# Late tiles of x loaded again in 32x32 blocks and turned by VectorE inside the scan, with their routing done pair by pair

## What is computed

```python
# layer 0, for each token (xf: x by token, tf: cond of its sequence)
shared = silu(xf @ w1) * (xf @ w3) @ w2
s = sigmoid(concat([xf, tf]) @ router_W)
_, topk_idx = top_k(s + router_bias, 2)
gates = s_sel / (s_sel.sum() + 1e-9)            # 1/2 each where the sum is not over 1e-9
y_e = gelu(xf @ W1e[e]) @ W2e[e]
x = x + (shared + sum of gates * y_e) / 3
# layer 1, for each step t of 512
Z = sigmoid(x_t @ Wxz.T + bxz + H @ Whz.T + bhz)
R = sigmoid(x_t @ Wxr.T + bxr + H @ Whr.T + bhr)
Ht = tanh(x_t @ Wxh.T + bxh + R * H @ Whh.T + bhh)
H = Z * H + (1 - Z) * Ht
x_t = x_t + H @ Whq.T + bhq
```

## Time and profile before

| | us |
|---|---|
| median of 3 runs | 1349.34 (1348.22 to 1351.28) |
| the profiled execution, whole | 1347.59 |
| its span | 1345.8 |
| PE busy | 1308.5 (97%) |
| DVE busy | 1015.7 (75%) |
| ACT busy | 806.8 (60%) |
| start of the scan, after the span's start | 88.78 |
| DMA | 43398 packets, 47.53 MB |
| granted TensorE clock | 0.998 of full speed |

### The profile page before, as it was taken

One profiled execution on the slowest core, in us unless ns is written; L12 is line 12 of the kernel. 1 busy time (PEld: TensorE's weight loads), 2 busy tenths in 40 slices (PEclk: granted clock), 3 DMA queues, 4 the chain that ended last, 5 costly groups with the idle time before them and its releaser, 6 DMA issues.

```text
span 1345.8 us, 82788 instructions
## 1 busy us (share of the span) xinstructions
PE 1308.5 (97%) x35358; PEld 880.8 (65%) x35358; DVE 1015.7 (75%) x5797; ACT 806.8 (60%) x4395; POOL 7.8 (1%) x26
## 2 busy tenths in 40 slices
PE   8989999999999999999999999999999999999877
PEld 7666666666666666666666666666666666666433
DVE  4458877787787778778777877778787877877755
ACT  4136666666666666666666666666666666666554
POOL 1000000000000000000000000000000000000000
PEclk9999999999999999999999999999999999999999
DMA  8410110101110010111101011110101011010110
GB/s 263 134 26 16 31 26 22 40 10 43 19 31 25 22 41 10 43 20 31 25 22 41 10 44 19 31 26 21 41 10 43 19 32 25 24 39 10 43 19 11
DMA packets 43398, 47.53 MB, mean 35 GB/s; under 512 B 7192, under 2 KB 38424, under 8 KB 43032
## 3 DMA queue, kind: packets, MB, share of 16 engines
q1 hardware_dynamic: 43032, 42.25, 12.4%
HBM read 25.46 MB, written 16.78 MB: 31 GB/s over the span
## 4 chain that ended last, share of the span: by engine, by line
PE 91%; DVE 4%; ACT 2%; SPq 1%; issue 1%; DMA 1%
PE up_ps L958 26%; PE zc_bank L1058 21%; PE dn_ps L931 21%; PE r_bank L1058 13%; PE aux L931 5%; PE misc L931 4%; DVE terms L832 1%; DVE t_rT L811 1%; ACT t_h L578 1%; ACT t_r L558 1%; DMA w_sb<-in_L_cond_w 1%; DVE hist L835 1%; SPq L362 0%; DVE rhT L814 0%; PE r_bank L883 0%
## 5 line engine op out<-in xcount | busy, mean ns | idle before, releaser
L578 ACT ACTIVATE t_h<-zc_bank 128x32 f32<-128x32 f32 x1024 | 146.2, 195 | 234.5 <-PE zc_bank L1058 234.5
L558 ACT ACTIVATE t_r<-r_bank 128x32 f32<-128x32 f32 x1024 | 146.2, 195 | 218.4 <-PE r_bank L1058 206.4
L931 PE MATMUL dn_ps<-we_sb,hid_e 128*32 128x256 f32 x4096 | 267.0, 379 | 1.4 <-DVE x_all L715 1.4
L1058 PEld LDWEIGHTS r_bank<-whT,hist 128*8 128x8 f32 x8192 | 117.4, 88 | 209.1 <-DVE hist L835 205.1
L811 DVE STREAM_TRANSPOSE t_rT<-t_r 128x32 f32<-128x32 f32 x1024 | 156.2, 191 | 108.0 <-ACT t_r L558 71.1
L832 DVE STREAM_TRANSPOSE terms<-t_h 128x32 f32<-128x32 f32 x1024 | 156.4, 192 | 96.3 <-ACT t_h L578 91.5
L1058 PE MATMUL r_bank<-whT,hist 128*8 128x64 f32 x8192 | 210.3, 220 | 13.5 <-DVE hist L835 11.8
L1058 PE MATMUL zc_bank<-whT,rhT 128*8 128x64 f32 x8192 | 211.2, 220 | 4.9
L1058 PE MATMUL zc_bank<-whT,hist 128*8 128x64 f32 x8192 | 209.4, 219 | 2.1 <-issue 2.1
L1058 PEld LDWEIGHTS zc_bank<-whT,rhT 128*8 128x8 f32 x8192 | 117.9, 88 | 89.5 <-DVE rhT L814 27.8
L958 PE MATMUL up_ps<-x_high,we_low 128*128 128x256 f32 x512 | 157.3, 307 | 0.0
(11 more groups left out here) (125 smaller groups left out, 1648.9 us busy)
## 6 DMA issues: line engine op xcount, KB each, us to landing
gate_inputs_by_token<-gru_raw SPq DMA_DIRECT2D x32, 384.0 KB, 2.4
gru_raw<-gate_inputs_by_token SPq DMA_DIRECT2D x256, 48.0 KB
x_all<-in_x SPq DMA_DIRECT2D x32, 128.0 KB
out<-gru_raw SPq DMA_DIRECT2D x32, 128.0 KB
x_all<-in_L_cond_W1e SPq DMA_DIRECT2D x1, 2048.0 KB, 11.0
we_sb<-in_L_cond_W2e SPq DMA_DIRECT2D x1, 2048.0 KB, 13.3
xT_all<-in_L_cond_w SPq DMA_DIRECT2D x2, 512.0 KB, 6.0
w_sb<-in_L_cond_w SPq DMA_DIRECT2D x1, 512.0 KB, 8.1
```

What stands on the lines that cost most here:

```text
L558: act.activation(t_r[:, i, :], r_ps[:, i * Q:(i + 1) * Q], ACT.Tanh, scale=0.5).then_inc(tr_ready, 1)
L578: act.activation(t_h[:, i, :], c_ps[:, i * Q:(i + 1) * Q], ACT.Tanh, scale=-1.0).then_inc(th_ready, 1)
L931: done = pe.matmul(ps[Q * j:Q * (j + 1), col:col + cols], lhsT[:, Q * j:Q * (j + 1)], rhs, start=first, stop=last, tile_position=(0, Q * j ...
L1058: done = pe.matmul(ps[Q * j:Q * j + B, :], lhsT[:, k, :], whT[:, gate, k, j * GW:(j + 1) * GW], start=False, stop=(k == NI - 1), tile_posi ...
```

## The change

**Loads.** SP loads the x of each tile from 4 on a second time, in blocks: for each of 4 channel groups, 2 parities of the sequence and 2 halves of the channels one DMA of 64 pieces of 128 B, 16 DMAs a tile, into x_blocks, which has room for two tiles (in xT_all, places 8 and 9). Tiles 4 and 5 are loaded in the head, behind the last load of x and before the wait for the first by_token store; tile n + 6 behind gate_rows(1) of tile n. The blocks are laid so that DVE's transpose of 32x32 blocks gives the turned tile.

**Turning.** late_xT is two DVE transposes of 128x128 for each tile, in the scan behind L835 at turns 2 and 7 (even tile) and 13 and 15 (odd tile), with a wait on the loads. xT_all keeps the late tiles in four places in rotation (place_xT).

**Logits and routing.** tile_logits: for each tile and half four float32 matmuls with 8 columns, on PE at turns 17 to 20, behind fill_rest's slots. add_base for the pair at turn 21 (DVE), score_tanh at turn 22 (ACT), the 25 routing operations on two tiles from turn 23 to turn 15 of the next span, on DVE between L817 and L827. This is done for 14 pairs.

**Removed.** The 14 groups of late transposes with their copies, rw_wide, late_logits, the two lgT copies and logits_by_token in the head; the one routing over 28 tiles in the first steps.

```diff
-            def late_logits():
-                ...
-                            last = pe.matmul(lg_ps[h][Q * j:Q * (j + 1), :], rw_wide[:, k, :],
-                                             xT_all[:, first_tile:first_tile + TG, k, :],
-                ...
-            def logits_by_token():
-                ...
+        LATE_XT2 = {2: (0, 0), 7: (0, 1), 13: (1, 0), 15: (1, 1)}
+        LOGITS2 = {17: (0, 0), 18: (0, 1), 19: (1, 0), 20: (1, 1)}
+        BASE1, TANH1, ROUTE1 = 21, 22, 23
+        BLOCK_LOADS = NG * 2 * KC
+        def place_xT(t):
+            return t if t < EARLY else EARLY + t % 4
...
+            def load_blocks(t):
+                for j in range(NG):
+                    for b in range(2):
+                        for k in range(KC):
+                            src = x[b::2, t * TS:(t + 1) * TS, k * P + Q * j:k * P + Q * (j + 1)].rearrange("i t c -> t i c")
+                            sp.dma_start(x_blocks[Q * j + TS * b:Q * j + TS * (b + 1), t % 2, k, :]
+                                         .rearrange("t (i c) -> t i c", i=NG), src).then_inc(ld_blocks[t % 2], 16)
+            load_blocks(EARLY)
+            load_blocks(EARLY + 1)
...
                     gate_rows(1, xs_second)
+                if EARLY <= n + EARLY + 2 < NT:
+                    sp.wait_ge(late_xT_ready, KC * (n + 1))
+                    load_blocks(n + EARLY + 2)
...
-                    if (n, s) == (0, LATE_SCORES + 1):
-                        score_tanh(1, slice(EARLY, NT))
+                    if EARLY <= 2 * p + 2 < NT and r == TANH1:
+                        score_tanh(p, slice(2 * p + 2, 2 * p + 4))
...
+            def late_xT(t, k):
+                dve.wait_ge(ld_blocks[t % 2], 16 * BLOCK_LOADS * ((t - EARLY) // 2 + 1))
+                dve.transpose(xT_all[:, place_xT(t), k, :], x_blocks[:, t % 2, k, :]).then_inc(late_xT_ready, 1)
...
+            def late_routing(p, r):
+                if r == BASE1 and EARLY <= 2 * p + 2 < NT:
+                    add_base(p, slice(2 * p + 2, 2 * p + 4))
+                ahead = 1 if r >= ROUTE1 else 0
+                first_tile, at = 2 * (p + ahead), (r - ROUTE1) % SPAN
+                if EARLY <= first_tile < NT:
+                    ops = route(slice(first_tile, first_tile + 2))
+                    if at < len(ops):
+                        ops[at]()
...
-                    if TS * n + s in ROUTE1:
-                        ROUTE1[TS * n + s]()
+                    late_routing(p, r)
...
+                    if r in LATE_XT2 and EARLY < 2 * p + 2 + LATE_XT2[r][0] < NT:
+                        late_xT(2 * p + 2 + LATE_XT2[r][0], LATE_XT2[r][1])
...
+            def tile_logits(t, k):
+                if k == 0:
+                    pe.wait_ge(late_xT_ready, KC * (t - EARLY + 1))
+                    if t % 2 == 0:
+                        pe.wait_ge(xp_ready, GATES * (t - 2))
+                done = product(misc, t % 2 * NE, NE, xT_all[:, place_xT(t), k, :], rw_sb[:, k, :], k == 0, k == KC - 1)
+                if t % 2 == 1 and k == KC - 1:
+                    done.then_inc(logits_done, 1)
...
+            set_bits()
+            for at in range(up_begin):
                 up(1, at)
-            for _ in LATE_TR[NSH]:
-                transposes(m)
-                m += 1
-            late_logits()
             for q in range(2):
                 for k in range(KC):
                     project(1, q, k)
-            pe.wait_ge(lgT_ready[0], 1)
-            pe.wait_ge(lgT_ready[1], 1)
-            set_bits()
-            logits_by_token()
```

More of the change, by code:

```diff
@@ L161, in moe_then_gru @@
         tr_dve = sem("tr_dve")
[L162 to L165, removed]
+        ld_blocks = [sem(f"ld_blocks{i}") for i in range(2)]
+        late_xT_ready = sem("late_xT_ready")
         logits_done = sem("logits_done")
@@ L244, in in_round @@
         def in_round(e):
[L246 removed]
+            sizes = [len(HEAD_TR)] + [len(r) for r in ROUND_TR]
             return range(sum(sizes[:e + 1]), sum(sizes[:e + 2]))
@@ L629, in score_tiles @@
                 dve.wait_ge(consts_ready, 1)
-                dve.wait_ge(score_ready, 1 if tiles.start == 0 else 2)
+                dve.wait_ge(score_ready, max(tiles.start // 2, 1))
                 link(dve.tensor_scalar(score[:, tiles, :], score[:, tiles, :], 0.5, 0.5, ALU.mult, ALU.add))
@@ L793, in _ @@
                 shared(1, u)
-                take_round(NE + u)
-            take_round(NE + NSH)
-            dve.wait_ge(lg_done, 2)
-            dve.tensor_copy(lgT[1], lg_ps[1][:, :]).then_inc(lgT_ready[1], 1)
+            for k in range(KC):
+                late_xT(EARLY, k)
             add_bias(1, 0)
             add_bias(1, 1)
-            ROUTE1 = dict(enumerate([lambda: add_base(1, slice(EARLY, NT)), *route(slice(EARLY, NT))], LATE_SCORES))
+            def late_routing(p, r):
[5 more added lines that the diff above has]
+                    ops = route(slice(first_tile, first_tile + 2))
+                    assert ROUTE1 - SPAN + len(ops) <= ADD2_ROUTED
+                    if at < len(ops):
+                        ops[at]()
             def body(n, scan, proj, outs):
@@ L1053, in fill_rest @@
                         keep_busy()
+                if r in LOGITS2 and EARLY <= 2 * p + 2 + LOGITS2[r][0] < NT:
+                    tile_logits(2 * p + 2 + LOGITS2[r][0], LOGITS2[r][1])
             def gate_product(ps, gate, lhsT, k):
@@ L1104, in _ @@
             up_begin = GAP1[SPAN - FIRST_STEP - TS].start
-            for place in range(NSH):
-                unit(1, place)
-                for _ in LATE_TR[place]:
-                    transposes(m)
-                    m += 1
-            for at in range(UP_MM * NSH, up_begin):
+            set_bits()
+            for at in range(up_begin):
                 up(1, at)
-            for _ in LATE_TR[NSH]:
-                transposes(m)
-                m += 1
-            late_logits()
             for q in range(2):
```

63 lines of the change are left out of this document (18 added, 45 removed).

## The result

| | before | after |
|---|---|---|
| median of 4 runs each | 1348.78 us (1348.01 to 1351.28) | 1378.87 us (1374.68 to 1382.14) |
| profiled execution | 1347.59, span 1345.8 | 1377.21, span 1375.4 |
| first r_bank of the scan | 88.78 | 78.94 |
| first to last L835 (L811 before), 512 steps | 1248.81 | 1288.25 |

The ratio is 1.0218, with a 95% interval of 1.0185 to 1.0251. The forecast was 1343.8 and faster, with a range of 1336 to 1354; the kernel became 30 us slower, which is outside the range. In the profiled executions the head gave back 9.8 us and the 512 steps took 39.4 us more.

What follows compares the result with a forecast made beforehand. It took the kernel as bound by the recurrence's loop of PE, ACT and DVE, 512 steps of about 2.43 us, not by matmuls alone. Head -15.0, DVE middle +7.8 and PE +1.7 sum to -5.5: median 1343.8 us, range 1336 to 1354.

Steps and rivals of the forecast that it cites:

- SP and the loads: DVE's wait for odd tiles' blocks at turn 13: 7.5 to 9.2 us against 8.8, so no stall; other end 5.
- doubled turns: Turns 3, 6, 7, 8, 10, 13, where routing joins another 256-wide DVE operation: 0.08 or 0.12 us late each.
- Rival 1: DVE waits for late blocks at turn 13, 13 times: 0.4 to 1 us each, centre 1352; chance 0.30.
- Head: Before the scan: removed work lets r_bank start at 73.8 instead of 88.78, gaining 15.0 us (12.5 to 15.6).
- Rival 3: Block loads in the head hold back by_token and xs_first; scan starts 9 us later than forecast, 1352.8; chance 0.05.
- DVE middle: Routing operations between L817 and L827: free alone, 7.8 us added in six turns a pair (2.5 to 17.6).
- rival 2: Pipe emptying behind each DVE operation makes the doubled middle cost 17 us instead of 7.8, 1353; chance 0.08.
- DVE end: Four 128x128 transposes a pair between L835 and the next L811, 0.36 us each: cost 0, at worst some 17.
- PE: Logits matmuls at turns 17 to 20 behind the filler L931: 1.7 us added (0 to 5.6).
- divisors 3.1 and 3.2: Used on PE's rows to space four matmul groups: 0.215 us a group for L931, 0.11 with 32 weight columns.
- 512 B: Skill page's minimum DMA size; below it SDMA reads, modifies and writes, so 128 B block pieces might land later.

Runs made afterwards that it cites:

- experiment 3: Changed kernel, 20 instead of 16 block loads per odd tile from 7: 1419.28 us. Columns: span, length, busy PE, PEld, DVE, ACT, POOL, clock share, DMA share, GB/s.
- experiment 1: Changed kernel with the same block loads issued for two tiles at once, behind the second gate rows of every even tile: 1343.73 us.
- experiment 4: Changed kernel with both 128-column halves of a block in one DMA, 8 loads of 128 pieces a tile instead of 16 of 64: 1339.78 us.
- experiment 7: Kernel of experiment 1 with SP's head reordered: block loads of tiles 4 and 5 first, load_x(3) behind the first gate rows: 1340.22 us.
- experiment 8: Kernel of experiment 1 with routing operations moved out of the doubled turns and the head order of experiment 7: 1336.09 us.
- experiment 9: Changed kernel with the merged loads of experiment 4 and routing operations moved out of the doubled turns, SP's order unchanged: 1335.38 us.
- Experiment 2: Changed kernel with the block loads of tiles 6 to 31 left out, all other operations done on old values: 1342.53 us.
- experiment 5: Changed kernel with the block loads of tiles 6 to 31 issued by GpSimd's queue instead of SP's: 1345.84 us.

## Why the prediction was wrong

*SP and the loads: "the middle, 8.3, fits: no stall".* This is the step that failed, and it carries nearly the whole error: 34.6 of the 35.1 us between forecast and result, with what hung on it; the other terms nearly cancel (the head 5.2 us worse than forecast, the doubled turns and the logits 4.2 better). The term that was mis-sized is the issue: 16 x 0.345 = 5.5 us was forecast, and 8.0 to 11.7, in the mean 9.7, was measured. Two things are in it. An undisturbed issue of this shape takes 0.43 us and 0.04 of gap, 16 x 0.47 = 7.5; I had taken the price from the gate rows because they have two levels as well, though their pieces are of 768 B and these of 128 B. And 60 of the 416 issues of the scan, 2.3 a tile, took 1.38 us on average, 2.3 x 0.95 = 2.2 more. Of the other two terms one was right and one too dear. The room behind the gate rows was forecast as 8.8. It was 8.7 ahead of ten of the 13 waits, 7.9 in the place shown above (gate rows of 2.08), and 9.4 and 9.8 in two places with irregular turns ahead: 8.75 in the mean. The landing was reckoned at 2.0 to 3.65 behind the end of the last issue; VectorE went on behind it after 1.2 to 1.4 us in ten places and 2.4 to 2.8 in three, 1.6 in the mean. So 9.7 + 1.6 - 8.75 = 2.6 us a tile, where 5.5 + 2.8 - 8.8 = -0.5 was forecast.

*Rival 1* was the right mechanism, with its place (turn 13), its count (13) and its sign in the waits view named. It was given 0.4 to 1 us each by the cheap price and 4.4 each by the dear price of x's loads, with centre 1352. The measured 2.6 each lies between. By the prediction's own sum, 13 x 2.6 - 5.5 = 28 us slower; it was 30. That these are so near is partly luck: the waits sum to 33.5 where the turns grew by 34.6, and the other terms made -4.5, not -5.5. The 0.345 should have been one end of a range of 0.345 to 0.7 an issue, whose middle already gives 8.4 us of issues and a stall of over 1.5 us, and no "fits". The range was made narrow by the choice of one similar row.

*What hung on the wait* was not in the forecast at all: six of the 13 waits are followed by 3.4 us of TensorE at half clock. The six were 2.6 to 3.9 us long; two more of 2.7 and 3.6 had no half clock behind them, nor had the five of 1.4 to 2.1. Windows of the changed kernel around the wait that ended at 494.03, with the columns of experiment 3:

```profile
490.00:495.10 5.10, 3.00 (x89) 1.97 (x92) 2.27 (x16) 1.30 (x8) 0.00 (x0) 1.00 0.27 90
495.10:498.50 3.40, 3.40 (x53) 2.35 (x44) 1.94 (x13) 1.37 (x8) 0.00 (x0) 0.50 0.00 0
498.50:503.00 4.50, 4.50 (x134) 2.90 (x134) 2.74 (x18) 2.68 (x15) 0.00 (x0) 0.99 0.02 4
```

TensorE was busy for 3.0 of 5.1 us, then had half its clock (1.2 GHz) for 3.4 us, then the full one. Turns 14 and 15 cost 0.32 and 0.21 more on average than in the kernel before, 13 x 0.53 = 6.8 us. Turn 13 itself grew by 13 x 2.14 = 27.8 beside its doubling, 0.44 each less than the waits, since VectorE stands at that place anyway: in experiment 1, without a wait, its next transpose L836 waits 0.46 us for t_r (at 484.06). Together 34.6. In the profiled executions the 512 steps of experiments 1 and 4 are 31.9 and 34.5 us shorter; the medians, which hold the heads too, are 35 and 39 lower.

*Head.* Forecast r_bank 73.8, measured 78.94. TensorE's own work was right: from xproj ready to r_bank it takes 8.65 to 8.68 us where nothing else is late (experiments 4, 7, 8 and 9), and 65.23 + 8.68 = 73.9. The measured 78.94 is this plus 3.2 (xproj later, in an execution with the long stretch at half clock) and 1.9 (SP's store late: issued at 70.97 instead of 68.4, r_bank idle 1.75). The second is the same mis-priced issue again: 32 loads should have ended at 63.1 and ended at 70.9, 6.5 us of it by the issues (17.52 instead of 11.04) and 1.4 because the loads of x ended at 53.4 and not at 52.0. Rival 3 had this mechanism and gave it 9 us at 0.7 an issue.

*DVE middle.* Forecast 7.8, measured 5.3. The spacings read from rows held: L855 stands 0.09 behind L850 (490.70 and 490.79). Turns 3 and 10 cost 0.09 where 0.12 was forecast, turn 8 nothing where 0.08 was, since in the kernel before it was already long. The Trainium skill, page "VectorE: DVE Perf Modes", section "The DRAIN you can't avoid", says that the next operation does not start until the pipe is empty, but also that one that is not held starts earlier. The prediction took up the first alone, as rival 2, and reckoned 17 from it. The rows show again an operation of 0.38 with the next one 0.30 behind its start (490.20 and 490.50), and the time followed the rows.

*DVE end.* The 128x128 transposes take 0.29 to 0.31 us (0.36 was the estimate) and cost nothing where the data is there: turns 2 and 15, which hold one each, have the medians 2.573 and 2.434 in experiment 1 and 2.573 and 2.433 in the kernel before.

*PE.* Forecast 1.7, measured 0. Turn 17 of the changed kernel:

```profile
503.68 1.05 PE L932 MATMUL dn_ps<-we_sb,hid_e 128*32 128x256 f32 x16
504.54 0.23 PE L932 MATMUL misc<-rw_sb,xT_all 128*32 128x8 f32 x8
504.65 0.41 PE L1071 MATMUL r_bank<-whT,hist 128*8 128x64 f32 x16
```

The eight logits matmuls start at 504.54 and r_bank at 504.65, 0.97 behind L932's start; in the earlier trace rows it was 0.98 without them. Turns 17 to 20 have a median of 2.43. The prediction's divisors 3.1 and 3.2 for the spacing of four groups have no source; with 3 the spacings are 0.22 and 0.12, and no term moves by more than 0.1 us.

*512 B.* The page "DMA: Bandwidth & Descriptors" of the Trainium skill was brought in as a reason for late landing. The page of the changed kernel's profile has a median of 2.0 us from issue to landing for the block loads, and 2.4 for the by_token stores, of 384 KB each; so no lateness of the small pieces shows there. Experiment 2 found no price of the traffic. What the loads do cost shows in the issue: 64 pieces 0.43 us, 128 pieces 0.60, and a by_token store 0.34 to 0.42 but for one slow one. Whether the size of a piece or another part of the shape sets this price was not tested.

The sum with measured terms, for the profiled executions: head -9.8, waits and clock behind them +34.6, doubled turns +5.3, logits 0: +30.1, measured +29.6.

The time of experiment 1, 1343.7, is nearly the forecast 1343.8. That is partly luck: its head gave 11.9 instead of 15, and its doubled turns cost 5.3 instead of 7.8 and the logits 0 instead of 1.7.

## What to carry to other kernels

Where a change puts many small DMAs between a queue's last duty and the first reader, price one issue by its own shape, and if no row has it, let the range run from the cheapest to the dearest row of that queue; a fit by less than the spread of these rows is no fit. And where single issues are slow now and then, as here, the median row is too cheap for a sum. Ask first whether the loads can stand elsewhere in the queue: here the same loads two tiles at a time, or half as many of twice the pieces, made a change of +2.2% into one of -0.3% and -0.6%. And a wait on the path of a recurrence can cost more than its length, when TensorE runs at half clock behind it: 27.3 us more of waits in experiment 3 made the scan 43.1 us longer.

## What the runs showed of the hardware

**Issues that take three times as long.** In the changed kernel the median block load takes 0.43 us to issue, but 60 of the 416 in the scan take over 0.8, on average 1.38 and up to 2.0. 53 of these 60 overlap in time with one of the 282 packets of 16 KB by which instructions are fetched (one every 4.8 us, 1.1 us each); of the 356 others 33 do. At random, by an estimate from these lengths, about half of the 60 would, and a third of the others. With the merged loads it is 25 of the 26 issues over 0.8 us, and 28 of the 182 others. So the two go together. But a fetch alone does not make an issue slow: in experiment 5, 139 of GpSimd's 416 issues overlap with one and none took over 0.64 us, and of SP's 256 gate rows in the changed kernel 88 overlap and 7 of these took over 0.6. No run changed the fetching alone, and the cause stays open. The queues of one tile's loads, in the window from 483 to 493 (packets, MB, share):

```profile
q1 hardware_dynamic: 1416, 0.27, 16.3%
q8 instruction: 2, 0.03, 1.3%
```

Two fetches in 10 us, and the DMA engines were busy for less than a fifth of the time, so they were far from full. One of the four gate rows at 481.27 is such a slow issue, 1.07 us beside a fetch from 481.34 to 482.29; it makes them 2.08 instead of 1.31. In the changed kernel the slow issues add some 1 us for each 4 to 5 us of block loads, by their number (60 in 26 x 9.7 us).

**Turns that stop for no seen reason.** All kernels, the one before too, have a few turns of 2.8 to 4 us where nothing of the change waits. In some of them TensorE stands about 1 us with "issue" as the releaser, which means that the profile shows nothing that it waited for, as here in experiment 1:

```profile
949.10 0.23 PE L1072 MATMUL r_bank<-whT,hist 128*8 128x64 f32 x2 [0.98 <-issue]
```

There are five such turns in the kernel before, two of them with a stop of TensorE of 1.0 and 1.2 us; six in experiment 1, two of them with 1.0 and 1.1; three in experiment 4; four in experiment 7. Some are the same turn of the same pair in several kernels (pair 12, turn 11; pair 5, turn 12). The cause stays open.

**A head that varies.** Between 22 and 32 us the profiled executions of kernels with the same work on TensorE there had 0, 3.4 or 6.8 us and more at half clock, and xproj came at 65.2 to 69.1. A term of a few us that is read from one profiled head is no surer than that.
